# First linear attention of a four-layer stack: one 32x32 matmul for each block of 32 tokens, and another order of the whole program

## The reference

```
HEADS = 8
BLOCK = 32
q, k, v = (to_blocks(q), to_blocks(k), to_blocks(v))
qp = jax.nn.elu(jnp.einsum('bhcsd,hdf->bhcsf', q, proj)) + 1.0
kp = jax.nn.elu(jnp.einsum('bhcsd,hdf->bhcsf', k, proj)) + 1.0
kv = jnp.einsum('bhcsf,bhcsd->bhcfd', kp, v)
num = jnp.einsum('bhcsf,bhcfd->bhcsd', qp, kv)
ksum = kp.sum(axis=3)
z = 1.0 / (jnp.einsum('bhcsf,bhcf->bhcs', qp, ksum) + 1e-08)
out = num * z[..., None]
```

## Time and profile before

| | us |
|---|---|
| Median of 3 runs | 1274.31 |
| Lowest and highest of them | 1266.7, 1274.86 |
| The profiled execution | 1260.86 |
| Its span (first to last instruction) | 1259.1 |

### The profile page before, as it was taken

The page is one execution under the profiler, slowest core; times in us unless marked ns, Lnnn a source line. Parts: engine busy times, 40 slices in busy tenths (PEclk is TensorE's granted clock), DMA queues, the critical chain, the costliest instruction groups (busy, mean ns, idle before and its releaser), DMA issues.

```text
span 1259.1 us, 15646 instructions
## 1 busy us (share of the span) xinstructions
PE 1128.0 (90%) x5494; PEld 714.2 (57%) x5494; DVE 902.0 (72%) x2074; ACT 697.0 (55%) x1167; POOL 510.6 (41%) x482
## 2 busy tenths in 40 slices
PE   7999999899999999999999776899998978639977
PEld 6765544355445574655544323597776746318967
DVE  4856437556658857779799998685688799956554
ACT  4575666876735755745676544653424777425221
POOL 2322123212225220065238455663276366584372
PEclk8999999999999879999999875898999989659999
DMA  8500000000000000000000000425323302046673
GB/s 266 194 1 1 1 1 0 1 1 1 1 17 1 1 1 1 18 1 1 1 1 1 0 0 17 149 87 180 126 82 101 109 16 97 16 127 217 236 254 118
DMA packets 39838, 76.86 MB, mean 61 GB/s; under 512 B 3281, under 2 KB 29009, under 8 KB 39249
## 3 DMA queue, kind: packets, MB, share of 16 engines
q0 software_dynamic: 10688, 51.39, 11.9%
q1 hardware_dynamic: 29072, 24.48, 6.1%
HBM read 65.30 MB, written 10.55 MB: 60 GB/s over the span
## 4 chain that ended last, share of the span: by engine, by line
PE 55%; DVE 13%; ACT 11%; POOL 10%; issue 6%; DMA 5%; POOLq 0%; SPq 0%; DVEq 0%; ACTq 0%
PE ps L894 7%; PE ps L2161 5%; PE ps L1469 4%; PE ps L2169 3%; PE ps L1278 2%; DVE own L2027 2%; PE ps L1287 2%; PE ps L668 2%; DMA g_f<-w,slot 2%; PE ps L856 2%; POOL sx L2414 2%; POOL own L2051 2%; PE ps L654 2%; POOL own L2446 1%; PE ps L1589 1%
## 5 line engine op out<-in xcount | busy, mean ns | idle before, releaser
L894 PE MATMUL ps<-own,g_f 128*128 128x512 f32 x320 | 146.1, 597 | 1.1 <-DVE own L1103 1.1
L1221 POOL TENSOR_TENSOR own<-own 128x512 f32<-128x512 f32 x32 | 43.4, 1355 | 162.4 <-PE ps L894 92.1
L894 PEld LDWEIGHTS ps<-own,g_f 128*128 128x128 f32 x320 | 59.1, 191 | 66.8 <-issue 58.4
L2027 DVE TENSOR_TENSOR_SCAN own<-own,carry 128x512 f32<-128x512 f32 x48 | 77.2, 1608 | 20.4 <-POOL own L2051 17.1
L2051 POOL TENSOR_TENSOR own<-own 128x512 f32<-128x512 f32 x32 | 51.9, 1622 | 77.6 <-ACT own L1977 77.6
L1931 PE MATMUL ps<-own,g_c 128*128 128x512 f32 x64 | 45.2, 795 | 40.7 <-POOL own L2057 40.5
L2238 ACT ACTIVATE own<-ps 128x512 f32<-128x512 f32 x60 | 35.7, 596 | 79.6 <-PE ps L2161 79.0
L1968 ACT ACTIVATE own<-own,Acol 128x512 f32<-128x512 f32 x64 | 45.2, 714 | 56.4 <-PE ps L1931 56.2
L2352 DVE TENSOR_TENSOR own<-ps,own 128x512 f32<-128x512 f32 x60 | 41.1, 684 | 47.1 <-PE ps L2161 40.2
L526 ACT ACTIVATE own<-xs,sm 128x128 f32<-128x128 f32 x128 | 52.5, 482 | 31.1 <-POOL sm L518 31.0
L1887 POOL TENSOR_TENSOR own<-own 128x512 f32<-128x512 f32 x32 | 43.6, 1365 | 55.4 <-DVE own L1861 51.7
(11 more groups left out here) (480 smaller groups left out, 3095.3 us busy)
## 6 DMA issues: line engine op xcount, KB each, us to landing
sx<-brow SPq DMA_DIRECT2D x4, 960.0 KB, 10.4
so<-own SPq DMA_DIRECT2D x11, 256.0 KB, 5.0
own<-sx SPq DMA_DIRECT2D x10, 256.0 KB, 4.8
g_l<-p_l SPq DMA_DIRECT2D x1, 2449.0 KB, 13.6
g_f<-p_f SPq DMA_DIRECT2D x1, 2223.5 KB, 9.1
own<-cs SPq DMA_DIRECT2D x8, 256.0 KB, 3.0
g_l<-p_l SPq DMA_DIRECT2D x1, 1866.0 KB, 10.9
g_l<-t_wmod SPq DMA_DIRECT2D x1, 1152.0 KB, 10.3
```

The costliest lines, as they stand in the source:

```text
L894: x = e.matmul(s.bank["V%d%d%d" % (it, k, cc)][:, :], ew2[:, m, 128 * cc:128 * cc + 128], gm, start=False, stop=m == 3)
L1221: e.tensor_tensor(R.gm[m % 2], R.g[m], R.mask[k][m], ALU.mult).then_inc(*s.pool.up("m%d%d%d" % (it, k, m)))
L2027: e.tensor_tensor_scan(H, A, H, init, ALU.mult, ALU.add).then_inc(*s.dve.up("H%d" % n))
```

## The change

Scores: where one matmul made 128 x 128, four now make the four diagonal blocks, 32 x 32 each over 128 features. Block b of group i goes to partitions 32b to 32b+31 and columns 32i to 32i+31 of the bank, so the scores of 512 tokens are 128 x 128 instead of 128 x 512, with no unwanted entry. The column group of the array follows from the partitions that are written. Mix: where one matmul had a contraction of 128, four have one of 32, each with a 32x32 weight in its own rows and columns of the array (the diagonal of the 4x4 grid of 32x32 parts). DVE: the masked multiply of 128 x 512 is a copy of 128 x 128. The mask's input is still loaded.

```
             def scores(hd):
...
                 for i in range(4):
-                    m = e.matmul(tl(p, i), tl(kf, i), tl(qf, i), start=True, stop=True)
+                    for b in range(4):
+                        at = 128 * i + 32 * b
+                        m = e.matmul(p[32 * b:32 * b + 32, 32 * i:32 * i + 32], kf[:, at:at + 32], qf[:, at:at + 32], start=True, stop=True)
                 m.then_inc(*s.pe.up("s%d" % hd))
             def mix(hd):
...
                 for i in range(4):
                     o = 17 * i if hd == 7 else 119 * i + 17 * hd
-                    m = e.matmul(p[:, o:o + 17], tl(b, i), vx[:, i, hd, :], start=True, stop=True)
+                    for k in range(0, 128, 32):
+                        m = e.matmul(p[k:k + 32, o:o + 17], b[k:k + 32, 32 * i:32 * i + 32], vx[k:k + 32, i, hd, :], start=True, stop=True)
                 m.then_inc(*s.pe.up("n%d" % hd))
...
-                e.tensor_tensor(tile4(T[c][8 + hd % 2]), tile4(s.bank["s%d" % hd][:, :]), V["block"].unsqueeze(1).broadcast_to([128, 4, 128]), ALU.mult).then_inc(*s.dve.up("s%d" % hd))
+                e.tensor_copy(T[c][8 + hd % 2][:, 0:128], s.bank["s%d" % hd][:, 0:128]).then_inc(*s.dve.up("s%d" % hd))
```

The schedule is another one throughout: all 42 lines of `ORDER` differ. Its first lines, before and after:

```
-    "tyytyojkkkopopeppplfmaoomaflrrfoalmnqarfqnafnrqoaahsokaaqqkksekkkkfrsgskskkfieacofoeffhoaaaahokkeykaccfkkkaafhdkfckiaaio"
+    "yokkjokotppyepppftyolaaoflfqqqqqoaomoafnagaamaanrkfskkrbklbkgkknmsffkagafkkbrffsakksiaakrrskaakbkfgdiakkfaakfagafbkkahkl"
```

More of the change, by code:

```diff
@@ L38 @@
[L38 to L45, removed]
@@ new lines @@
+    "ccggkhhchcckmpmcpmcmppcfmmccdmmhbhcnllcjjlclhhchcmccmhbhcgbbcygbhgcgcbmlhbblarlfbdmbplpbbgamaagblllgkagmnbfrrbbllafflrfr"
+    "aakfhkakakfkbffclaahldtlalnfbnngknikikbbddkgkagdngafanffbffbadlalfbnbbakggakbfpkkddibkndddnkanknafliakakdifakdkfaafadiii"
+    "daagqkallaapaklqqaaqqpaaafffdddknfndngdkndkndinddifakkndnnpdiaapdadiiiddeoooddfddfnfdnnnndnfddibidkkddikgdkdikdknaanniki"
+    "dnddnfaafaaffaiidkfdkdikddkpidaniaasafnqqfaafkaflafbfbbbgbtggbblllllaagaggfaaapafaaaffnaknfsskssbpkkkkibaagkgdakiglllllb"
@@ new lines @@
+    "bpfaafaafaaffkbkbakkgkggkpbbaakgpgglbblalllblbblbgqbbgbbgbgbblglllbfbflffbbfqbkkbbbkqblkbgkgkbgkkgbaqlaglblflaflbqfaaaaf"
+    "gakgkgkfagkrccrckhkcmlhhpchlppcclpclfclhhphlmlmabhbmfbmgmagkagfkafbfaaffgbbgcchcbmmfmkmfaflffmfclchclkhhccbbhcqfkklcbhff"
+    "khchbmrhmmgmcbbcmghlmgmcgcmamhfamhmfccfcccfafmffcaakrfkkkfccfkmckkfrfhkaaaahfbffahkfkkaaffffkahcaffkkckccckmcbhrmgmmafmr"
+    "gccffcffakfkkabbakahfkkbfkafbkhbbakbbgabbhkqgggbglhlblblmqlalbllmmambbbkbqgbbmkkggkkagmfblmgalqbbkkkblpplplpflcclchqafhc"
@@ new lines @@
+    "sdimmmrniididdlllllndnniwwnssdidniiirrnddwrwvnrdnrscnhcshnicdhnidnnddiidciccsinhcshnccchdnnddddimmcnrcciiisniscmhncccnrh"
+    "ndmdimdcmniiiicrsccncsmchnicchrncmsdmmcrdmncchdnnccrccnhssmwcmsmcsimrccschcrdiccmdmhnncnicncccnrnnnhdmccccmnnnnrnwnhnnmc"
+    "ccnsssnmnnnsrnhcdinsdidimnddimmcdmnccnchncdimdmddididnnnccwcndhdimddididnnnccsnddimmddisdidnnnsdnsssdisddididnnwrndnddix"
+    "xdidsndddixnndidnsddnndindddnnsdidsdnddinndiddddximnsdmnndddidndnndmddndnidndnddmmddddddwinnnddinnddnnndnnnx"
```

56 lines of the change are left out of this document (26 added, 30 removed).

## The result

| | before | after |
|---|---|---|
| Median, us (20 runs each, alternating on one chip) | 1271.09 | 1276.72 |
| Lowest and highest, us | 1256.14, 1275.39 | 1269.63, 1284.06 |
| Ratio of after to before, 95% interval | | 1.0063, 1.0037 to 1.0090 |
| Profiled execution, its span, us | 1260.86, 1259.1 | 1284.06, 1282.3 |

The forecast was 0.9% less; it is 0.6% more, within the 1% I called no change, inside the range, and of the other sign. Ratios here are worked out from single executions, without those over 1.5% above the fastest of their kernel (one of the new matmuls under the old order took 3680.33 us), so they can differ by up to 0.3% from the ratio of two medians.

A forecast was written before the change was run, and what follows sets the result against it. PE was taken to set the pace where the changed part mostly runs (240 to 560 us). The terms -22 + 11 + 0 + 0 = -11 us took the median 1274.3 to 1263 us, 0.9% less; range 1244 to 1287.

The forecast's parts named there:

- What bounds the kernel: PE sets the pace from 240 to 560 us, DVE from 560 to 780; what PE saves is saved.
- Term 1: Scores and mix on PE: 64 groups at 0.55 us instead of 0.89, -22 us, between -43 and 0.
- fully parallel: Rival for scores and mix: groups of 0.22 to 0.35 us, about -22 us in all, 1252 us; chance 0.14.
- Term 2: Turns between parts of PE's array, 0.09 us each plus the exposed load: 24.7 us before, 35.5 now, +11 us.
- DVE: Eviction of scores from 687 to 280 ns, 13 us less on DVE, counted as 0; the shorter eviction keeps it hidden.
- The new order: The new schedule moves PE's neighbours by a few groups; set at 0, with +-8 us for the range.
- The clock: Rival: PE loses full clock in six further stretches of 8 us, +24 us, sum +13, 1287 us; shared chance 0.20.
- down by some 10 us: Sign that the forecast is right: PE's busy time over the kernel falls by some 10 us.

The follow-up runs named there:

- e1_tiles_old_order: The changed kernel with the old ORDER string, so new small matmuls and short eviction under the old schedule: 1246.82 us, 0.9931 of the kernel before.

## Why the prediction was wrong, step by step

**What bounds the kernel: half right.** PE did set the pace from 240 to 560 us, but "what PE saves is saved" failed after the first ten us. With the old order PE was 28 to 37 us less busy in four traces and the time fell by 9 (1255.77 to 1246.82). The mix alone, 11 us off PE, reached the same time. PE had 7 us of idle time in a window of 320, and DVE and ACT were at 220 and 201: averages that look roomy. After some ten us the waits between the engines bind. Which of them (I suspect the chain of a head: maps, elu on ACT and DVE, scores, eviction, mix) no run separated.

**Term 1: right mechanism, wrong size.** I took 0.55 us a group, halfway between full parallel work (0.22) and no gain (0.89); measured 0.25 to 0.30. With 0.26 term 1 is 64 x (0.26 - 0.89) = -40 us instead of -22, with 0.28 it is -39. The row that I leaned on for feeding, pairs every 26 ns, was not the feeder's rate, since groups now start a pair every 8 to 9 ns; the row of L1271's loads pointed the right way. The rival *fully parallel* had the group right (0.22 to 0.35), and still promised 22 us where the matmuls brought 9. The Trainium skill, page "TensorEngine Tiling (Array Packing)", section "Performance Considerations", gives every matmul about 60 cycles of its own, by which I had estimated 0.80 us a group. This case's traces do not agree: small matmuls in changing parts of the array are started as a pair every 8 to 9 ns.

**Term 2: right.** In after a turn is 0.09 us (L858 ahead of the scores, 0.95 - 0.86) and the load of 128 columns behind one 0.10 (L856 at 277.47, 0.96 - 0.86); for 64 columns it is 0.06 (L863 in `e1_tiles_old_order`, 1.01 from 455.75 to 456.76, less 0.86 and the turn of 0.09; I had 0.05 without a row), and the 0.03 for 32 columns stands in the earlier trace rows. Terms 1 and 2 now give -40 + 11 = -29; PE's busy time fell by 28.0 and 31.2 in the first two traces with the old order (29.3 and 37.2 in the others), whose 211 turns are nearly those of the new order.

**DVE: right in the sum, wrong in the reason.** The eviction is 285 ns, and its length is worth nothing that can be measured. But the short copy is not what hides it, as I had written: at 685 ns it was hidden too.

**The new order: the step that failed.** "I set the order at 0, with +-8 for the range." It costs 11 to 14 us with the old matmuls (1.0112), 0.5% with the new ones on chips of 1256 us, and some 1.5% on the others (1.0063 and 1.0093 against 0.9921, each from another chip). But for the 0.5% that is more than the 8 us that I allowed, and with only 9 us from the matmuls it turned the sign on chips like that of the result; on chips of 1256 us the two cancel (0.9981, 1.0008). The chips differ by the stall: it costs 14 us with the new matmuls under the old order and 22 under the new one. I had priced one place, and there the priced wait did go. The timeline of PE in after, against the earlier trace rows, and the windows against the earlier trace rows:

```profile
449.89 0.65 PE L1599 MATMUL ps<-g_c,own 128*128 128x128 f32 x4
450.84 0.66 PE L1280 MATMUL ps<-own 128*32 128x32 f32 x32 [0.30 <-DVE xs L1206]
451.42 0.62 PE L1290 MATMUL ps<-vext,own 32*32 32x17 f32 x32
...
454.96 3.18 PE L856 MATMUL ps<-own,g_f 128*128 128x512 f32 x4
457.98 1.05 PE L1605 MATMUL ps<-g_l,own 128*128 128x128 f32 x8
```

```profile
448.00:452.00 4.00, 3.62 (x79) 2.20 (x78) 3.52 (x7) 3.94 (x8) 1.16 (x2) 0.82 0.00 0
452.00:456.00 4.00, 4.00 (x72) 1.72 (x69) 3.34 (x14) 3.89 (x7) 1.96 (x3) 0.50 0.01 4
456.00:460.00 4.00, 3.80 (x76) 2.39 (x74) 0.92 (x2) 3.98 (x8) 1.17 (x4) 0.82 0.00 0
```

The product finds its operand ready (no idle time ahead of L1605), but 18 us later than before (457.98 against 439.81), and the half clock came anyway: a shorter stretch there (0.50 from 452 us, 0.82 before and behind it), and another ahead of it, with 0.66 from 400 to 440 us where the kernel before has 0.87. Chunk 0's L2A ends at 459 us instead of 442. By itself even that cost little: with the new order to letter 2030 the ratio is 0.9969. The loss that is best shown is where I did not look, from 550 to 750 us. I had written that no changed instruction stands there and that DVE sets the pace; I should have compared the two orders there first, because an engine that sets the pace can lose by every wait that a new neighbourhood puts ahead of it.

**The clock** did not turn the sign: 240 to 560 us has 0.94, as before. From 780 to 860 us it is 0.76 to 0.79 in the two traces of the changed kernel with the stall, 0.87 and 0.89 in the two without, and 0.88 before. With the new matmuls and the old order it is 0.68 to 0.77 from 400 to 440 us, but 0.91 to 0.95 over the whole of 240 to 560.

**PE's busy time, "down by some 10 us",** came out at 9.8, by accident. In the two traces of the same kernel without the stall it is down by 22.7 and 26.1, near the -29 of the terms as measured; the two with the stall have 12 to 16 us more of it, in its lumps and at the lower clock around them.

## What to carry to other kernels

Small matmuls that go round different parts of the array are cheap here (8 to 9 ns a pair), and a turn with the load behind it costs 0.12 to 0.20 us: count turns as well as matmuls. When an engine is 7 us in 320 short of full, it need not stay the bound: here the first 11 us taken from it came through, the next 20 did not. Ask what chain runs beside it before you book the rest. And time a change and a new schedule apart: here the matmuls with the old order (0.992 to 0.995 of before in four measurements, or 0.992 with the mix alone) beat both kernels, and the new schedule gave the gain away.

## What the runs showed of the hardware

A group of 32 pairs on the diagonal 32x32 parts takes 0.25 us, one of 32 pairs with 128 rows by 32 columns 0.27 to 0.30 us, both without the turn. On the chips where the kernel before has a median of 1268 us or more, PE, DVE and ACT are held up together for some 10 us between 775 and 850 us and for up to 16 us near the end, while POOL starts indirect DMAs; on the two others none of ten traces shows it, with the same kernels and the same DMAs. Between the medians this is 14 or 15 us of 1256, and 22 with the new order. A DVE copy out of PSUM of 128x128 is 285 ns and one of 128x512 685 ns, the same as with a multiplication in it (280 and 687).
